# Raw second-layer weights requested before the zero fills, two start-up fills moved from VectorE to GpSimd, and activation tables touched early

## The chip, the core and the metric

The kernel runs on one core of a Trainium2 chip. The metric is the device time of one execution in microseconds, as the median of several runs. Beside the timed runs there is one profiled execution, from which every row below comes.

## The reference, cut to what matters

The input is `x` of 16 batches of 256 tokens with 128 channels, all in float32. Two layers follow one another. Each is "modulate, attention-like block, add back, modulate, expert block, add back".

```python
# layer 0, attention: 16 heads of 8 channels, causal softmax, a gate per token
logits = where(causal, einsum('bqhd,bkhd->bhqk', Q, K) * scale, -inf)
out = einsum('bhqk,bkhd->bqhd', softmax(logits) * gate, V) @ Wo + bo
# layer 0, expert block: plain attention over 256 tokens, then 8 experts, all used for every token
y = einsum('bse,bseh->bsh', softmax(x @ Wg + bg), relu(x @ W1 + b1) @ W2 + b2)
# layer 1, linear attention, with qkv_w, p1_w, p2_w (the "raw second-layer weights", used transposed)
kv = einsum('bhqd,bhqe->bhde', layernorm(k), layernorm(v)) / Q * temperature + attn_bias
h = gelu((q @ kv + x) @ p1_w.T + p1_b) @ p2_w.T + p2_b + x
# layer 1, expert block: top 2 of 8 experts with a capacity of 1024 slots each; rows beyond it are dropped
h = gelu(xb @ w1) @ w2        # xb: the rows gathered by slot; results are added back by token
```

## The kernel before, in words

All of the work is cut into named steps, such as `("up", n, e, f)`. A small planner inside the kernel file (`Plan`, `order_steps`) simulates the engines with a guessed cost for every part of a step (`work="sp:10 dma:6"` means ten microseconds of SyncE's queue and then six of a transfer), and writes down for every engine the order in which the parts were taken. The program of each engine is then those parts in that order. Each engine works strictly in its order and waits on semaphores in front of each part, so an early part that has to wait holds up all behind it. In the planner a part becomes available when all steps in its `after` have ended, 0.2 after the last of them. TensorE takes the available part of lowest rank. Every other queue takes the one with the smallest value of (time at which it became available minus `urgent`). Transfers don't compete with each other in the planner.

```python
for entry in sorted(queue, key=lambda q: (q[2].rank, q[1]) if ranked
                    else (q[0] - q[2].urgent, q[2].rank, q[1])):
```

The steps that matter here, in order of time:

- **Start.** VectorE fills the four `k_stack` tiles with -1 (`L1666`, semaphore `minus`), and only then begins its planned order with `moment(0)` (`L1739`), `stat(0,0,0)`, which needs the first quarter of `x` (`L1007`). GpSimd builds the constants and, in `masks()`, the causal masks (`L2520`).
- **Layer-0 attention.** ScalarE, VectorE (chunk 0) or GpSimd (later chunks, `L2589`, `L2594`) cut the projections into three bfloat16 pieces (`L1796` to `L1800`). SyncE writes them to memory (`write`, `L1047`) and reads them back in another layout (`stack(b, w)`, `L1059`; w = 0 is q, w = 1 is k). `max` (`L1247`, `L1263`) is the first TensorE work of a batch. `mrow(b)` sends the row maxima to the stack (`L1066`). `exp` and `pv` follow. Batch `b` uses tile `b % 4`.
- **Fills.** Four transfers zero the answer rows (`L1088`) and four the routed rows (`L1091`), about 1 MB each: steps `bg 4` to `bg 11`. The following SyncE parts are `wraw` (the raw second-layer weights, `L1098` to `L1100`), `mg_w(0)` (the first chunk's gate rows, out of `gT`, written to memory, `L1111`), `blk` (32 tiny transfers, `L1106` and `L1107`), `w1` (2 MB of expert weights, `L1128`) and `mg_r(0, 0)` (the gate rows read back, spread over the partitions, `L1122`). `mg_w(n)` first waits for `mg_t(n)`, ScalarE's copy into `gT` (`L2397`).
- **Layer-0 experts.** `up` (`L1454`), `down` (`L1487`), then `mix(n, e)` on VectorE (`L1965`), which needs the gate rows and frees a PSUM bank, and `acc` on GpSimd (`L2633`). Between them run the plain attention steps of later chunks and `wt(0)` to `wt(4)`, the transposes of the raw weights (`L1530`), then `wc` on VectorE. All of them are needed only by layer 1.
- **Layer 1.** Linear attention of chunk n overlaps the layer-0 experts of later chunks: `la_1` (`L2473`, Gelu), `la_2` (`L1582`), `la_c` (`L2479`), `la_x` (`L1590`); `rt_e` (`L2485`, Exp) begins the routing. When ScalarE's next function isn't in the table that is loaded, an ACT_TABLE_LOAD stands before the activation.

Of the kernel before, what the change touches and what calls it, by code (L numbers as in the profile page):

```python
# [12 lines left out]
ACT = mybir.ActivationFunctionType  # L13
# [3 lines left out]
B, S, C = 16, 256, 128  # L17
P = 128
# [10 lines left out]
NCH = TOK // CHUNK  # L29
CT = CHUNK // P  # L30
BPC = CHUNK // S
# [15 lines left out]
QR = 4  # L47
# [297 lines left out]
def order_steps():  # L345
    p = Plan()
# [88 lines left out]
    ROWS_AT = 9  # L435
    for b in range(B):
        for w in range(2):
            p.step("stack", b, w, work="sp:1.4 dma:2.0", urgent=3 if b < 2 else 0, after=[("write", b // BPC, w, b % BPC)]
                   + ([(("exp", b - QR, u), "pe") for u in range(6)] if b >= QR else []))
        for u in range(6):  # L440
            pair = p.buffer("pair")
            p.step("max", b, u, work=f"pe:{.52 if u < 2 else .42} dve:1.2", urgent=8 if b == 0 else 2, after=[("stack", b, 0), ("stack", b, 1), ("masks",)] + ([(("mrow", b - 2), "pe")] if b >= 2 else []), rank=10 * (6 * b + u - ROWS_AT) + 3,
                   opens=[(0, pair)], closes=[(1, pair)], pair=pair)
        bank = p.buffer("bank")
        p.step("mrow", b, work="pe:.32 act:.32 dve:.42 sp:1.15 dma:2.2", urgent=9 if b < 2 else 6, after=[("max", b, u) for u in range(6)]
               + ([("mrow", b - 2)] if b >= 2 else []), rank=10 * (6 * b - 4), opens=[(0, bank)], closes=[(2, bank)], bank=bank)
        for h in range(2):
            sums = p.buffer("bank")
            for v in range(3 * h, 3 * h + 3):
                u, pair, probs = EXPS[v], p.buffer("pair"), p.buffer("probs")  # L450
                p.step("exp", b, u, work=f"pe:{.42 if u < 4 else .52} act:.93", after=[("mrow", b)], rank=10 * (6 * b + v),
                       opens=[(0, pair), (0, probs)], closes=[(1, pair)], pair=pair, probs=probs)
                p.step("pv", b, v, work="pe:.5", after=[("exp", b, u), ("gv_v", (TPB * b + u // 4) // GT)]
                       + ([("pv", b, v - 1)] if v % 3 else []), rank=10 * (6 * b + v + 2) + 5,
                       opens=[(0, sums)] if v % 3 == 0 else [], closes=[(0, probs)], sums=sums, probs=probs)
            tile, bank = p.buffer("turned"), p.buffer("bank")
            p.step("oc", b, h, work="act:.53", after=[("pv", b, 3 * h + 2)], opens=[(0, tile)], closes=[(0, sums)], sums=sums,
                   turned=tile)
            p.step("turn", b, h, work="pe:.5 dve:.45", after=[("oc", b, h)], rank=10 * (6 * b + 3 * h + 6) + 1, opens=[(0, bank)],
                   closes=[(0, tile), (1, bank)], bank=bank, turned=tile)  # L460
# [17 lines left out]
    values_over = [gated, *[("gv_a", n) for n in range(NT // GT)]]  # L478
# [13 lines left out]
        p.step("free", n, work="sp:0", after=[("values_over",)], opens=[(0, t) for t in tiles])  # L492
        p.step("bg", n, work="sp:.8 dma:10", after=[("free", n)], first=tiles[0], second=tiles[1])
    for n in range(4, 12):
        p.step("bg", n, work="sp:.8 dma:9", after=[("mrow", B - 1)])


    def project_out(n, rank, chain):
# [79 lines left out]
    for e in range(NE):  # L578
        p.step("sw", 0, e, work="act:.53 dve:.62",
               after=[("bg", 0), ("bg", 1), last_pv] + [(("exp", 12 + e // 2, u), "pe") for u in range(6)])  # L580
# [27 lines left out]
        p.step("w2", h, work="sp:.5 dma:4", after=[(("down", NCH - 1, 2 * h + 1, FC - 1), "pe")]  # L608
               + ([("fetch", u) for u in range(2)] if h == 3 else []))

    p.step("wraw", work="sp:10 dma:6", after=[*values_over, ("mrow", B - 1)])
    for g in range(5):
        one("wt", g, "pe:.12 dve:.22", [("wraw",)], MOE - 60, (91, g, 0))
    p.step("wc", work="dve:2.5", after=[("wt", g) for g in range(5)] + [("mod", 1)])
# [122 lines left out]
def build(nc, a, out):  # L737
    ctx = ExitStack()
    with ctx:
        def sb(name, shape, dt=F32):  # L740
            return ctx.enter_context(nc.sbuf_tensor(name, shape, dt))

        def semaphore(name):
            return ctx.enter_context(nc.semaphore(name))

        p = order_steps()
# [3 lines left out]
        def sem(kind, by=None):  # L750

            stage, engines = SIGNALS[kind]
            return stage_sems[stage, by or engines.split()[-1]]
# [8 lines left out]
        def held(name, *step):  # L762
            return p.held[step, name].at
# [36 lines left out]
        def pair_of_tiles(i):  # L800
            if i < 4:
                return tmp[:, 2 * i:2 * i + 2, :]
            if i >= 8:
# [28 lines left out]
        result_out = semaphore("result_out")  # L832
        consts = semaphore("consts")
        IDENT, COUNTERS, ZEROS, VA_PAD, VA_ONES, EMPTY, MASKS = range(1, 8)
        minus = semaphore("minus")

        wqk = sb("wqk", [P, 2, C])
        wvd = sb("wvd", [P, VW])
# [1 line left out]
        magic = sb("magic", [P, 1])  # L840
        mixed_bias = sb("mixed_bias", [P, 1])
        least = sb("least", [P, 1])
        wo = sb("wo", [P, C])
        fw = sb("fw", [P, 4, C])
        wg = sb("wg", [P, NE])
# [8 lines left out]
                  for wh in range(2)]  # L854

        PLACES = ((slice(0, 3), slice(3, 6, 2), slice(4, 5)), (slice(2, 5), slice(0, 6, 5), slice(1, 2)))
        q_heads, k_heads = ([t[:, :, :].rearrange("p a t -> p (a t)").bitcast(BF16).rearrange("p (i t) -> p i t", i=IH)
                             for t in stacks] for stacks in (q_stack, k_stack))
# [16 lines left out]
        def col(name, i=0):  # L875
            return cols[:, COLS[name] + i:COLS[name] + i + 1]
# [126 lines left out]
        def _(eng):  # L1003
            w = Waits(eng)
# [45 lines left out]
            def stack(b, wh):  # L1050
                r, n = b % QR, b * S // CHUNK
                dst, src, sem_in = ((q_heads, q_pieces, q_in), (k_heads, k_pieces, k_in))[wh]
                w.wait_ge(minus, 1)
                if b >= QR:
                    for u in range(6):
                        w.wait_ge(*done("exp", b - QR, u, by="pe"))
                w.wait_ge(piece_out[wh][b % BPC], 16 * 3 * (n + 1))
                for j in range(2):
                    eng.dma_start(dst[r][HALF * j:HALF * j + DEEP, :, :].rearrange("p i t -> p (i t)"),  # L1059
                                  src[n, b % BPC, :, :, j, :, :].rearrange("s d i t -> (s d) (i t)")).then_inc(sem_in[r], 16)  # L1060
# [599 lines left out]
        def _(eng):  # L1660
            w = Waits(eng)
            chain = Tally(semaphore("vector_chain"))


            for r in range(QR):
                last = eng.memset(k_heads[r][:, :, :], -1.0)  # L1666
            last.then_inc(minus, 1)

# [18 lines left out]
                return eng.scalar_tensor_tensor(y, t, 1.5 * 0.375, y, ALU.add, ALU.mult)  # L1687

            eng.memset(least[:, :], EPS)
            eng.memset(magic[:, :], float(0x5F3759DF)).then_inc(chain.sem, chain.more())  # L1690
            w.wait_ge(chain.sem, chain.n)

# [534 lines left out]
        def _(eng):  # L2227
            w = Waits(eng)

            for name, at in COLS.items():  # L2230
# [5 lines left out]
                n = v.shape[0] // P  # L2236
# [232 lines left out]
            def la_1(b):  # L2469
                w.wait_ge(*done("la_1", b, by="pe"))  # L2470
                for c in cleared("tmp", "la_1", b):
                    w.wait_ge(*c)
                eng.activation(T(held("tmp", "la_1", b))[:, 0:S], psum[:, held("bank", "la_1", b), 0:S], ACT.Gelu,  # L2473
                               bias=col("L1_attn_p1_b")).then_inc(sem("la_1"), 1)

            def la_c(b):
                t = T(held("src", "la_c", b))[:, 0:S]
# [4 lines left out]
            def rt_e(g):  # L2482
                t = sc[:, g * RG:(g + 1) * RG, :]
                w.wait_ge(*done("rt_s", g))
                eng.activation(t, t, ACT.Exp).then_inc(sem("rt_e"), 1)  # L2485

            def rt_b(b):
                r = b % 2
# [26 lines left out]
        def _(eng):  # L2515
            w = Waits(eng)
# [15 lines left out]
            for t in range(NT // 8):  # L2532
                last = eng.memset(va[:, 8 * t:8 * t + 8, :, HD], 1.0)
# [5 lines left out]
            def masks():  # L2539
# [19 lines left out]
                for stage in stages:  # L2559
                    w.wait_ge(chain.sem, chain.n)  # L2560
                    for j in range(2):
                        last = stage(slice(HALF * j, HALF * (j + 1)))[-1]
                    if stage is not stages[-1]:
                        last.then_inc(chain.sem, chain.more())
                last.then_inc(consts, 1)
                w.wait_ge(consts, MASKS)

            def late():
                eng.dma_start(wo[:, :], a["L0_attn_Wo"]).then_inc(late_in, 16)
# [173 lines left out]
```

## Time and profile before

| | |
|---|---|
| median of 3 runs | 1013.37 us (1011.25 to 1015.28) |
| the profiled execution's own time | 1019.3 us |
| its span, first to last instruction | 1017.5 us |
| TensorE busy with matmuls | 936.2 us, 92% |
| VectorE, ScalarE, GpSimd busy | 608.9, 567.8, 347.9 us |
| mean granted TensorE clock | 0.963 |

The profiled execution is 1.8 us longer than its own span, and 5.9 us longer than the median. Times in the rows count from the start of the span. "Idle before" is the time that an engine had nothing to do just before an instruction, and the arrow names what ended it.

### The profile page before, as it was taken

Reading aid. Unit: us, or ns where it says so; the run is one execution under the profiler, and the core shown is the slowest. Engines: PE = TensorE matmul, PEld = TensorE weight load, DVE = VectorE, ACT = ScalarE, POOL = GpSimd, SP = SyncE. Lnnn points to the kernel's source line nnn. Section 1 sums busy time; section 2 is a strip of 40 time slices with the busy share of each in tenths; the row PEclk is TensorE's granted clock in tenths of the full one; section 3 lists DMA queues with packets and bytes.
Section 4 is the critical chain, followed back from the end, with each engine's and each line's share of the span. In section 5 each row is a group of like instructions: output and inputs, shape, how many; then the busy total and the mean of one; then the engine's idle time right before and its main releaser. Section 6 shows DMA issues by size and latency. Waiting matters only on the chain.

```text
span 1017.5 us, 17056 instructions
## 1 busy us (share of the span) xinstructions
PE 936.2 (92%) x6324; PEld 628.5 (62%) x6324; DVE 608.9 (60%) x1747; ACT 567.8 (56%) x965; POOL 347.9 (34%) x436
## 2 busy tenths in 40 slices
PE   4599889888988999999999999999999998988997
PEld 3355555545656787656666566666666666877983
DVE  8988778577475675355554535554455764747334
ACT  4477876775774565445465455545555565453430
POOL 4446540330000000233424443243533323457671
PEclk9599999989997999999999999999999998998999
DMA  5865342643593000101101111111101213112316
GB/s 136 205 156 133 101 122 66 157 123 141 123 226 125 23 22 3 43 21 52 53 22 63 42 40 44 47 37 42 62 21 53 73 47 97 44 50 72 107 46 227
DMA packets 86398, 83.10 MB, mean 82 GB/s; under 512 B 9202, under 2 KB 72680, under 8 KB 86316
## 3 DMA queue, kind: packets, MB, share of 16 engines
q1 hardware_dynamic: 81092, 73.32, 26.1%
q0 software_dynamic: 4320, 8.27, 2.5%
q8 instruction: 50, 0.82, 0.3%
q10 hardware_dynamic: 904, 0.42, 0.1%
q14 instruction: 32, 0.26, 0.1%
HBM read 50.53 MB, written 31.72 MB: 81 GB/s over the span
## 4 chain that ended last, share of the span: by engine, by line
PE 56%; DVE 13%; issue 10%; ACT 9%; SPq 5%; POOL 5%; DMA 2%; another core or an unknown queue 0%; POOLq 0%; DVEq 0%; ACTq 0%
PE psum L1454 13%; PE psum L1487 12%; PE psum L1477 4%; PE psum L1309 4%; PE psum L1247 3%; PE psum L1263 2%; PE psum L1290 2%; POOL routed L2691 2%; SPq L1091 2%; ACT ew L2323 1%; PE psum L1217 1%; PE psum L1239 1%; POOL hT L2633 1%; DVE maxes L1844 1%; PE psum L1368 1%
## 5 line engine op out<-in xcount | busy, mean ns | idle before, releaser
L2432 ACT ACTIVATE big<-psum,cols 128x512 f32<-128x512 f32 x256 | 173.8, 689 | 162.7 <-PE psum L1454 152.1
L1454 PE MATMUL psum<-parts,q_stack 128*128 128x512 f32 x640 | 260.2, 488 | 4.2 <-issue 2.3
L1487 PE MATMUL psum<-big,ew 128*128 128x512 f32 x512 | 249.5, 595 | 0.0
L2633 POOL TENSOR_TENSOR hT<-hT,gb_tok 128x512 f32<-128x512 f32 x56 | 73.6, 1315 | 289.5 <-DVE gb_tok L1965 289.1
L1454 PEld LDWEIGHTS psum<-parts,q_stack 128*128 128x128 f32 x640 | 113.4, 194 | 61.7 <-issue 50.1
L1844 DVE TENSOR_REDUCE maxes<-psum 128x4 f32<-128x1024 f32 (+1 forms) x96 | 114.8, 1218 | 27.6 <-PE psum L1263 27.3
L1487 PEld LDWEIGHTS psum<-big,ew 128*128 128x128 f32 x512 | 96.1, 190 | 53.2 <-issue 39.9
L1454 PE MATMUL psum<-parts,k_stack 128*128 128x512 f32 x320 | 127.5, 398 | 0.0
L1965 DVE SCALAR_TENSOR_TENSOR gb_tok<-psum,cols,gb_tok 128x512 f32<-128x512 f32 x64 | 47.9, 749 | 92.4 <-PE psum L1487 84.7
L2714 POOL DMA_INDIRECT answers<-hT,to x64 | 62.5, 976 | 54.7 <-DVE hT L2163 38.0
L2691 POOL DMA_INDIRECT routed<-big,slot_i x64 | 63.2, 988 | 41.8 <-DVE slot_i L2143 22.2
L1477 PEld LDWEIGHTS psum<-ew,big 128*128 128x128 f32 x512 | 67.8, 200 | 9.4 <-issue 3.2
L1477 PE MATMUL psum<-ew,big 128*128 128x128 f32 x512 | 68.9, 284 | 4.7 <-issue 2.6
L2439 ACT ACTIVATE big<-psum 128x512 f32<-128x512 f32 x64 | 38.2, 598 | 56.9 <-PE psum L1454 39.8
L1454 PEld LDWEIGHTS psum<-parts,k_stack 128*128 128x128 f32 x320 | 61.1, 191 | 13.9
L2323 ACT ACTIVATE ew<-psum 128x1024 f32<-128x1024 f32 x60 | 60.6, 1023 | 13.5 <-PE psum L1290 12.7
L2255 ACT ACTIVATE hT<-psum,modT 128x256 f32<-128x256 f32 x64 | 34.5, 565 | 33.9 <-PE psum L1217 33.7
L1247 PE MATMUL psum<-mask_qk,rows_qk 64*128 64x128 bf16 (+1 forms) x384 | 33.6, 256 | 21.2 <-DMA k_stack<-k_pieces 7.5
L2633 POOL TENSOR_TENSOR hT<-big,gb_tok 128x512 f32<-128x512 f32 x8 | 10.2, 1278 | 107.8 <-DVE gb_tok L1965 107.7
L2589 POOL TENSOR_TENSOR ew<-ew,gb_tok 128x512 f32<-128x512 f32 x14 | 16.1, 1155 | 85.6 <-ACT ew L2288 85.6
L2163 DVE TENSOR_SCALAR hT<-psum,big 128x128 f32<-128x128 f32 x64 | 18.4, 345 | 42.9 <-PE psum L1477 36.2
L1309 PE MATMUL psum<-ew,big 128*32 128x128 f32 (+1 forms) x640 | 41.2, 355 | 1.5 <-ACT ew L2323 1.1
(401 smaller groups left out, 1656.2 us busy)
## 6 DMA issues: line engine op xcount, KB each, us to landing
gb_tok<-gate_rows SPq DMA_DIRECT2D x32, 512.0 KB
q_stack<-q_pieces SPq DMA_DIRECT2D x32, 192.0 KB, 3.5
k_stack<-k_pieces SPq DMA_DIRECT2D x32, 192.0 KB, 4.5
routed<-empty_row SPq DMA_DIRECT2D x4, 1040.0 KB, 13.4
big<-routed SPq DMA_DIRECT2D x16, 260.0 KB
answers<-gb_tok SPq DMA_DIRECT2D x4, 1024.0 KB, 11.1
q_pieces<-gb_tok SPq DMA_DIRECT2D x16, 192.0 KB, 2.1
k_pieces<-gb_tok SPq DMA_DIRECT2D x15, 192.0 KB, 2.1
```

The lines of the kernel that those rows point to most:

```text
L1247: eng.matmul(bank(2 * s + j).rearrange("p (g k) -> p g k", k=width)[:, :, cs], rows_of[rs, half, :], mask[rs, 0:heads, :], start=half == 0 ...
L1309: last = eng.matmul(psum[QUAD * c:QUAD * (c + 1), bank_at, (g % 2) * S + kb * P:(g % 2 + 1) * S], va_flat[:, TPB * b + kb, at:at + QUAD], ...
L1454: last = eng.matmul(bank(i), w1_part(wp, e)[:, fs], parts[2 * xk + xp][:, :], start=n == 0, stop=n == 2)
L1477: last = eng.matmul(psum[:, i, k * C:(k + 1) * C], hid[:, r, f, k * P:(k + 1) * P], ew2[:, e, f, :], start=f == 0, stop=f == FC - 1)
L1487: eng.matmul(bank(i), ew2[:, e, f, :], hid[:, r, f, :], start=f == 0, stop=f == FC - 1).then_inc(sem("down", "pe"))
L1844: eng.tensor_reduce(maxes[:, b % 2, qb, :, ii[0]:ii[-1] + 1], psum[:, 2 * s:2 * s + 2, :].rearrange("p j (g k) -> p j g k", k=P * (qb + 1) ...
L1965: eng.scalar_tensor_tensor(tile, bank(held("bank", "mix", n, e)), col("L0_ffn_b2", e), tile, ALU.add, ALU.mult).then_inc(sem("mix"), 1)
L2323: eng.activation(pair_of_tiles(held("probs", "exp", b, u)), psum[:, 2 * s:2 * s + 2, :], ACT.Exp, scale=float(HD) ** -0.5).then_inc(sem("e ...
L2432: eng.activation(hid[:, held("hid", "up", n, e, f), f, :], bank(held("bank", "up", n, e, f)), ACT.Relu, bias=col("L0_ffn_b1", e * FC + f)) ...
L2633: eng.tensor_tensor(hT[:, ns], xpT[:, ns] if e == 0 else hT[:, ns], gate_wide[:, e // GHELD % 2, e % GHELD, :], ALU.add).then_inc(sem("acc ...
L2691: eng.indirect_dma_start(out=routed, out_offset=bass.IndirectOffsetOnAxis(ap=slot_i[:, k, t:t + 1], axis=0), in_=rows_buf[:, r, m, k, :], ...
L2714: eng.indirect_dma_start(out=answers, out_offset=bass.IndirectOffsetOnAxis(ap=to[:, k, m:m + 1], axis=0), in_=ans_buf[:, k, m, :], in_offs ...
```

## The change

Four things are changed.

1. `wraw` is planned with 1.5 instead of 10 microseconds of SyncE and with `urgent=20`, and each of the eight fills has `wraw` in its `after`.
2. The stacks of batch 0 have `urgent=9` instead of 3.
3. The fill of `k_stack` tiles 2 and 3 goes from VectorE's beginning to the end of GpSimd's `masks()`. It has a semaphore of its own, `minus_later`, on which the stacks of these two tiles wait.
4. ScalarE runs a two-element Exp after each odd `la_1` but the last, and a two-element Gelu after `rt_e(0)` to `rt_e(5)`, on a new small tile `ready`.

```diff
-            p.step("stack", b, w, work="sp:1.4 dma:2.0", urgent=3 if b < 2 else 0, after=[("write", b // BPC, w, b % BPC)]
+            p.step("stack", b, w, work="sp:1.4 dma:2.0", urgent=9 if b < 1 else 3 if b < 2 else 0, after=[("write", b // BPC, w, b % BPC)]
...
     for n in range(4, 12):
-        p.step("bg", n, work="sp:.8 dma:9", after=[("mrow", B - 1)])
+        p.step("bg", n, work="sp:.8 dma:9", after=[("mrow", B - 1), ("wraw",)])
...
-    p.step("wraw", work="sp:10 dma:6", after=[*values_over, ("mrow", B - 1)])
+    p.step("wraw", work="sp:1.5 dma:6", urgent=20, after=[*values_over, ("mrow", B - 1)])
...
+        ready = sb("ready", [P, 2])
...
-                w.wait_ge(minus, 1)
+                w.wait_ge(*((minus, 1) if r < BPC else (minus_later, 1)))
...
-            for r in range(QR):
+            for r in range(BPC):
                 last = eng.memset(k_heads[r][:, :, :], -1.0)
             last.then_inc(minus, 1)
...
+            eng.memset(ready[:, :], 0.0)
...
                                bias=col("L1_attn_p1_b")).then_inc(sem("la_1"), 1)
+                if b % BPC == BPC - 1 and b < B - 1:
+                    eng.activation(ready[:, 1:2], ready[:, 0:1], ACT.Exp)
...
                 eng.activation(t, t, ACT.Exp).then_inc(sem("rt_e"), 1)
+                if g < NCH - 2:
+                    eng.activation(ready[:, 1:2], ready[:, 0:1], ACT.Gelu)
...
                 w.wait_ge(consts, MASKS)
+                for r in range(BPC, QR):
+                    last = eng.memset(k_heads[r][:, :, :], -1.0)
+                last.then_inc(minus_later, 1)
```

Here `BPC` is 2, `QR` is 4, `B` is 16 and `NCH` is 8.

## Rows read from the trace of the kernel before

**Rows 1.** The page, part 1: busy time, share of the span, instructions.

```profile
span 1017.5 us, 17056 instructions
...
PE 936.2 (92%) x6324; PEld 628.5 (62%) x6324; DVE 608.9 (60%) x1747; ACT 567.8 (56%) x965; POOL 347.9 (34%) x436
```

**Rows 2.** Timeline 0 to 60 us: start, duration, engine, line, out<-in, [idle before <-releaser].

```profile
1.71 0.45 SPq L1007 DMA_DIRECT2D x<-in_L_attn_x  x1
...
2.28 0.73 POOL L2531 MEMSET big<- 128x736 f32 x1
...
9.56 0.49 DVE L1739 BATCH_NORM_STATS2 stats<-x 128x6 f32<-128x128 f32 x2
...
20.13 0.69 DVE L1796 TENSOR_TENSOR ew<-ew,gb_tok 128x512 f32<-128x512 f32 x1 [0.68 <-ACT ew L2288]
...
26.84 1.80 SPq L1059 DMA_DIRECT2D q_stack<-q_pieces  x4
...
29.02 2.27 POOL L2589 TENSOR_TENSOR ew<-ew,gb_tok 128x512 f32<-128x512 f32 x2 [15.41 <-ACT ew L2288]
29.11 1.09 DVE L1672 SCALAR_TENSOR_TENSOR drs<-drift,magic 128x8 int32<-128x8 int32 x1
...
35.67 0.61 PE L1247 MATMUL psum<-mask_qk,rows_qk 64*128 64x256 bf16 x4 [7.52 <-DMA k_stack<-k_pieces]
```

**Rows 3.** Instructions on tile k_stack: durations in ns min/median/max, first and last start.

```profile
L1666 DVE MEMSET k_stack<- x4: 1765/1765/1765, 1.3 to 7.7; 128x2048 bf16 x4
```

**Rows 4.** DMA issues, window 0 to 2.15 us: KB each, us from issue to landing.

```profile
x<-in_L_attn_x SPq DMA_DIRECT2D x1, 512.0 KB, 4.5
```

**Rows 5.** Timeline 262 to 330 us, all engines.

```profile
278.13 0.57 ACT L2397 COPY gT<-psum 8x512 f32<-8x512 f32 x1
...
304.28 0.48 PE L1530 MATMUL psum<-ident,big 128*128 128x128 f32 x1 [4.05 <-DMA big<-in_L_attn_p_w]
...
321.55 0.75 DVE L1965 SCALAR_TENSOR_TENSOR gb_tok<-psum,cols,gb_tok 128x512 f32<-128x512 f32 x1 [4.33 <-DMA gb_tok<-gate_rows]
...
322.45 0.85 PE L1217 MATMUL psum<-ident,tmp 128*128 128x128 f32 x6 [1.50 <-DVE gb_tok L1965]
...
324.42 1.19 PE L1454 MATMUL psum<-parts,q_stack 128*128 128x512 f32 x2 [1.12 <-DVE x L1874]
```

**Rows 6.** Timeline of SyncE's queue, 200 to 420 us.

```profile
267.76 0.41 SPq L1088 DMA_DIRECT2D answers<-gb_tok  x1
...
289.83 4.79 SPq L1091 DMA_DIRECT2D routed<-empty_row  x1
294.67 3.54 SPq L1098 DMA_DIRECT2D big<-in_L_attn_qkv_w  x1
...
300.22 0.33 SPq L1111 DMA_DIRECT2D gate_rows<-gT  x1
...
311.67 0.40 SPq L1128 DMA_DIRECT2D ew<-in_L_ffn_w  x1
```

**Rows 7.** The chain that ended last, 260 to 335 us: start, duration, what.

```profile
312.17 9.27 DMA gb_tok<-gate_rows
```

**Rows 8.** Windows of 5 us: busy per engine, then TensorE clock, DMA share, GB/s.

```profile
305.00:310.00 5.00, 5.00 (x12) 3.19 (x11) 1.46 (x5) 1.08 (x3) 0.00 (x0) 0.50 0.02 1
...
325.00:330.00 5.00, 5.00 (x16) 4.03 (x15) 4.66 (x24) 3.57 (x8) 0.00 (x0) 0.50 0.01 3
```

**Rows 9.** Groups by line and form, ScalarE: busy us, mean ns, idle before.

```profile
L2473 ACT ACT_TABLE_LOAD x8 | 10.3, 1283 | 0.1
```

**Rows 10.** Timeline 445 to 530 us, around the first two linear-attention chunks.

```profile
452.08 0.70 PE L1582 MATMUL psum<-tmp,w_t 128*128 128x256 f32 x2 [0.84 <-ACT tmp L2473]
...
453.62 0.59 ACT L2479 ACTIVATE tmp<-tmp,small,modT 128x256 f32<-128x256 f32 x1
...
454.77 0.38 PE L1590 MATMUL psum<-ident,tmp 128*128 128x128 f32 x2
...
514.06 0.70 PE L1582 MATMUL psum<-big,w_t 128*128 128x256 f32 x2 [0.56 <-ACT big L2473]
```

More of the change, by code:

```diff
@@ L834, in build @@
         IDENT, COUNTERS, ZEROS, VA_PAD, VA_ONES, EMPTY, MASKS = range(1, 8)
-        minus = semaphore("minus")
+        minus, minus_later = semaphore("minus"), semaphore("minus_later")
         wqk = sb("wqk", [P, 2, C])
```

## The prediction, made before the result was known

> **What bounds the kernel now.** I read the page first. TensorE is busy for 936.2 of 1017.5 us [rows 1], and after the first 60 us it has few gaps, so a gap taken away or added there reaches the end nearly whole. The edits touch three stretches, and in each I looked for what ends the gap.
>
> At the start the timeline [rows 2] shows VectorE at work without a pause. Its first planned instruction is at 9.56, behind four fills of 1.765 us [rows 3]. TensorE stands still for 7.52 us until 35.67, when the k stack of batch 0 lands. The view of that chain runs back over SyncE's issues from 26.84 on and over the pieces to VectorE at 9.56: the beginning of VectorE sets it, not TensorE.
>
> At the fills there are two gaps. TensorE waits 4.05 us for the raw weights, until 304.28. Then VectorE's `mix(0,0)` waits 4.33 us for the gate rows and starts at 321.55, and TensorE has gaps of 1.50 and 1.12 us on its account [rows 5]. The second is the one that counts: the chain that ended last passes through SyncE's whole row of fills, raw weights and tiny transfers, and over the gate transfer, landing at 312.17 + 9.27 = 321.44 [rows 6, 7]. What TensorE loses to the raw weights is lost only until it has run out of work that doesn't need the gates. So the question for this stretch is when the gate rows land.
>
> In layer 1 the reader should see small gaps before `la_2`, 0.84 us in the first chunk, behind table loads of 1.283 us [rows 9, 10].
>
> **The change part by part.**
>
> *The first batch's stacks first.* In the planner SyncE is free at 23.81 and takes `stack(0,0)`. At 25.21 it is free again. Then `stack(1,0)` is available (since 24.91) and `stack(0,1)` isn't: its `write` ends at 26.02. The next choice, at 26.61, falls on `stack(0,1)` with either urgency. The order stays q0, q1, k0, k1, as the trace has it (two q stacks, four issues, from 26.84 before the first k stack) [rows 2]. Value 0. Had the order become q0, k0, k would be issued 0.9 us earlier (half of 1.80), which is the bound.
>
> *Two fills to GpSimd.* VectorE is free two fills earlier, each 1.765 plus 0.38 between them, 4.3 us in all; it would be ready at about 5.3. But `moment(0)` needs the first quarter of `x`, issued at 1.71 (issue 0.45) and landing 4.5 later [rows 2, 4]: 6.2 to 6.7, take 6.5. Gain 9.56 - 6.5 = 3.1. On GpSimd a fill of 736 elements takes 0.73 [rows 2], so 2048 take about 2.0, two of them 4.0, from 13.6 (29.02 - 15.41 [rows 2]) to 17.6. Its next work is then due at about 26, so nothing of GpSimd waits, nor do the stacks of tiles 2 and 3. VectorE could: a VectorE instruction that took 0.17 elsewhere took 1.09 beside GpSimd's tensor operation at 29.02 [rows 2]. VectorE's slack before the first cut into pieces is 0.68 (20.13 [rows 2]). The four fills of VectorE all took the same 1.765 although GpSimd filled beside only the first ones [rows 3], so I take 0.2 for contention and keep 2 fills of 2.0 less 0.68, 3.3, as its bound. Value -2.9, bounds -4.3 and +0.2. The `ready` fill is under 0.1.
>
> For this contention the Trainium skill ("SBUF — State Buffer", section "Who interferes with whom") has a rule: whichever starts first, a GpSimd operation or a VectorE copy or tensor_scalar in a two-port mode, holds the shared ports for the whole instruction, while tensor_tensor collides only with GpSimd's reads. By the rule a long fill on GpSimd could stop VectorE's copies for 2 us each, and the gain would be near 0; by the row of equal fills it is 2.9. The row at 29.11 agrees with the lock itself.
>
> *Raw weights ahead of the fills.* This needs the order of SyncE, which the planner fixes. In the planner of before `mrow(15)` ends at 240.13, the fills are taken from there, and `mg_w(0)` becomes available at 247.70. Nothing earlier changes, so these two stand. Now `wraw` is taken at 240.13: 1.5 of SyncE, 0.2, 6 of transfer, 0.2, ended at 248.03. The fills become available only then. `mg_w(0)` is available 0.33 before them, at an idle SyncE, and is taken first. The new order is therefore `wraw`, **`mg_w(0)`**, eight fills, `blk`, `w1`, `mg_r(0,0)`; before it was fills, `wraw`, `mg_w(0)`, `blk`, `w1`, `mg_r(0,0)`.
>
> On the chip `mg_w(0)` waits for ScalarE's copy into `gT`, which ends at 278.13 + 0.57 = 278.70 [rows 5] and depends on nothing that moved. Behind it on SyncE now stand all eight fills, which began at 267.76 [rows 6]. `wraw` alone takes three issues of about 0.45 with nothing queued, so SyncE is at the wait by 269.2 and stands there for 9.5 us. The count, all from [rows 6]:
>
> - The first fill moves from 267.76 to about 279.1: +11.3.
> - From the first to the end of the last fill it was 294.62 - 267.76 = 26.9, paced by the transfers. The same.
> - `wraw` and `mg_w(0)` no longer stand behind the fills: 300.55 - 294.67 = -5.9.
> - `blk` and `w1` as before.
>
> Sum +5.4: the gate rows are asked for at 317.6 instead of 312.17 and land at 326.9. The fills' landing isn't later than that: 267.76 to 304.2 was 36.5 us with the raw weights in it, so 279.1 + 35.5 = 314.6.
>
> The raw weights are there from about 275, and the 4.05 us gap goes, with the half-clock stretch behind it (0.50 in 305 to 310 [rows 8]). But TensorE then only runs out of work sooner, by some 6 to 7 us, and waits at the same place for gates that are 5.4 later. After the wait it has a half-clock stretch as it had before (0.50 in 325 to 330), so that cancels. Value of this part +5.4.
>
> *The order around it.* The planner believes that the gates come earlier: fills at 248.3 to 254.7, `blk` to 265.7, `mg_r(0,0)` at 265.8 instead of 268.2. So `mix(0,0)` becomes available about 1 earlier, at 273.1 instead of 274.2, and passes `stat(0,1,4)` (3.2 long in the planner, available at about 274). VectorE's order has `mix(0,0)`, and TensorE's the first step that needs its bank, with up to 5 us less of other work ahead of them. Each microsecond of such work that is moved behind the late gates is one more gap. From 0 to +5; I take +2, since banks and not VectorE often decide. The five transposes and `wc` go earlier and cost the same. The orders after this point are all shuffled; for that I add 3 us to either side.
>
> *Tables.* Without the load, `la_1` is 1.28 sooner. TensorE shows 0.84 of gap in the first chunk and 0.56 in the second [rows 10], and two more chunks have a gap like the second's. But `la_1(0)` follows the gates' Exp and keeps its load; only chunks 1 to 6 gain. The Exp after the odd `la_1` puts 1.28 + 0.2 on ScalarE where `la_c` of the even batch stands in half of the chunks: at 453.62 it started right after the odd `la_1`, and TensorE wants its result at 454.77 [rows 10]. It would come at 453.7 + 1.5 + 0.6 = 455.8, a gap of 1.0. So: chunks 1, 3 and 5 gain 0.8 each, 6 gains about 1; chunk 0 loses 1.0, chunks 2 and 4 lose 0.5 each: -3.4 + 2.0 = -1.4. Bounds: no loss, -4; no gain, +3. `rt_e` sooner by up to 1.28 meets no gap of TensorE.
>
> The Trainium skill ("ScalarE: Activation LUTs", section "What ACT_TABLE_LOAD costs") puts a switch at 2.66 us, load and drain. By it the gains and the losses here would double, to -2.8. The trace shows the load's 1.283 [rows 9] and the activation right behind.
>
> **The sum.** -2.9 + 5.4 + 2 - 1.4 = +3.1 us. On the profiled execution, 1019.3, that is 1022.4; on the median of the runs, 1013.37, it is 1016.5. A difference of 0.5%, 5.1 us, is about what a measurement of this kernel can tell.
>
> **The rivals.**
>
> - *The gates aren't late (faster).* If `mg_w(0)` stands behind the fills, SyncE loses 1.4 to `wraw` at the front and gains 5.5 behind: gates 4.1 earlier. With the start and tables: -4.1 - 2.9 - 1.4 = -8.4, 1005. The point that decides is 0.33 of planner time between `mg_w(0)` and the fills. My derivation excludes it, but a slip there is possible, or late gates that hit less work than I think.
> - *More work behind the gates (slower).* The reorder costs its 5 instead of 2, and the start gives only 1 because of GpSimd's fills: -1 + 5.4 + 5 - 1 = +8.4, 1022. For it: TensorE's gaps at 322 and 324 come directly from `mix(0,0)` and what is behind it. Against: with VectorE held up, much of the other work was already prepared.
> - *The start doesn't move.* The weights or the second quarter of `x` come too late; then +6.0, 1019.4. Against: TensorE waited 7.52 at 35.67 for this chain alone.
> - *All of it is hidden or cancels:* layer 1 absorbs the delay in its own gaps, within 2 us of 1013.4.
>
> **How the numbers follow.** Forecast (1012.5 to 1019, start gained, gates late) 0.46; gates not late 0.13; more work behind the gates 0.20; start unmoved 0.09; all cancels 0.12. The range reaches down to 1006, into the first rival, and up to 1024, past the second. Slower by over 0.5% begins at 1018.4: the second rival, most of the third and a part of the forecast's upper side, 0.36. Faster ends at 1008.3: the first rival and a little of the shuffle, 0.15. Same 0.49.
>
> **What would show it.** VectorE's first `L1739` at about 6.5, and TensorE's first `L1247` at about 32.8, still after q0, q1, k0, k1. SyncE: `L1098` at 267.8 - 2.9 = 265, `L1111` behind it at about 276, the first `L1088` after that. `L1530` with no gap. The first `L1965` at about 324, with over 7 us of VectorE's and TensorE's idle time before it. Eight `L2473` loads become two, and `L1590` has new gaps. The prediction is wrong if `L1111` stands behind the fills, or if TensorE has no long gap before the first `L1965`.

## The result, and the profile after

| | before | after |
|---|---|---|
| median of the runs | 1012.31 us (4 runs, 1011.23 to 1015.28) | 1024.27 us (4 runs, 1022.33 to 1025.69) |
| the profiled execution, its span | 1019.3, 1017.5 us | 1025.69, 1023.9 us |
| mean granted TensorE clock there | 0.963 | 0.968 |

The ratio is 1.0126, with a 95% interval of 1.0098 to 1.0155: the change makes the kernel 1.3% slower, 12 us. The forecast was 1016.5, that is 3.1 us slower, with a range of 1006 to 1024.

The two profiled spans differ by 6.4 us only. That of before was made in an execution 7 us above its median, so nothing below rests on the difference of these two spans. The kernel before was profiled a second time for that (first experiment). Line numbers shift by 1 or 2 with the change: `L1247` is now `L1248`, `L1454` `L1455`, `L1965` `L1967`, `L1111` `L1112`.

Page of the changed kernel, part 1, beside [rows 1]:

```profile
span 1023.9 us, 17061 instructions
...
PE 931.1 (91%) x6324; PEld 624.7 (61%) x6324; DVE 607.5 (59%) x1746; ACT 569.2 (56%) x978; POOL 351.9 (34%) x438
```

TensorE has the same 6324 matmuls and is no busier than before (931.1 us for 936.2). What was lost is idle time. The timeline of SyncE's queue, which answers to [rows 6] (start, duration, what is issued):

```profile
261.22 0.41 SPq L1099 DMA_DIRECT2D big<-in_L_attn_qkv_w  x1
...
262.20 0.44 SPq L1101 DMA_DIRECT2D big<-in_L_attn_p_w  x1
272.19 0.30 SPq L1112 DMA_DIRECT2D gate_rows<-gT  x1
272.53 0.40 SPq L1089 DMA_DIRECT2D answers<-gb_tok  x1
...
293.54 4.23 SPq L1092 DMA_DIRECT2D routed<-empty_row  x1
297.81 3.02 SPq L1107 DMA_DIRECT2D tcol<-in_L_attn_temperature  x1
...
311.77 0.39 SPq L1129 DMA_DIRECT2D ew<-in_L_ffn_w  x1
312.27 0.98 SPq L1123 DMA_DIRECT2D gb_tok<-gate_rows  x2
```

This is the order that the prediction had: raw weights, `mg_w(0)`, eight fills, `blk`, `w1`, gates. SyncE stands from 262.6 to 272.19 at the gate write (`L1112`), and the fills begin behind it. TensorE and VectorE, timelines, beside [rows 5]:

```profile
276.09 0.27 PE L1531 MATMUL psum<-ident,big 128*128 128x128 f32 x1
...
316.72 1.12 PE L1401 MATMUL psum<-ident,tmp 128*128 128x128 f32 x4 [12.79 <-DVE tmp L1909]
...
322.13 2.08 PE L1390 MATMUL psum<-tmp 128*128 128x256 f32 x4 [3.01 <-DVE gb_tok L1967]
```

```profile
312.68 0.29 DVE L1992 TENSOR_SCALAR wqk<-wqk,tcol 128x128 f32<-128x128 f32 x1 [14.22 <-DMA wqk<-in_L_attn_attn_bias]
...
321.32 0.75 DVE L1967 SCALAR_TENSOR_TENSOR gb_tok<-psum,cols,gb_tok 128x512 f32<-128x512 f32 x1 [4.66 <-DMA gb_tok<-gate_rows]
```

The first transpose of the raw weights no longer waits (4.05 us before). But TensorE has two gaps of 12.79 and 3.01 us on account of VectorE, which stands first at `blk` (`L1992`, 14.22 us), for the 32 tiny transfers, and then at `mix(0,0)` (`L1967`, 4.66 us), for the gates. Windows of 5 us, beside [rows 8] (busy us of TensorE, its weight loads, VectorE, ScalarE, GpSimd; then the granted clock):

```profile
305.00:310.00 5.00, 0.00 (x0) 0.00 (x0) 0.00 (x0) 0.00 (x0) 0.00 (x0) 0.92 0.02 0
310.00:315.00 5.00, 0.00 (x0) 0.00 (x0) 2.11 (x14) 0.00 (x0) 0.00 (x0) 0.50 0.37 114
315.00:320.00 5.00, 2.40 (x7) 1.58 (x7) 1.49 (x8) 1.27 (x2) 0.00 (x0) 0.50 1.03 381
320.00:325.00 5.00, 2.87 (x7) 2.33 (x8) 3.68 (x11) 0.00 (x0) 1.27 (x1) 0.50 0.35 141
325.00:330.00 5.00, 5.00 (x25) 4.34 (x24) 3.88 (x20) 2.92 (x9) 0.00 (x0) 0.88 0.00 0
```

For five microseconds no compute engine does anything, and the work behind the gap begins at the lower of the two clocks (0.50, 1.2 GHz).

### The profile page after: what moved, and what is told of

It is laid out like the page before. It is cut to its first block, busy times and chain, and to the rows that moved or that the text cites. A ratio compares the mean times of both kernels' runs of the same rounds, so it can differ in the third digit from the quotient of the medians.

```text
span 1023.9 us, 17061 instructions
## 1 busy us (share of the span) xinstructions
PE 931.1 (91%) x6324; PEld 624.7 (61%) x6324; DVE 607.5 (59%) x1746; ACT 569.2 (56%) x978; POOL 351.9 (34%) x438
## 4 chain that ended last, share of the span: by engine, by line
PE 58%; DVE 13%; issue 9%; ACT 8%; SPq 4%; POOL 4%; DMA 3%; another core or an unknown queue 0%; DVEq 0%; POOLq 0%; ACTq 0%
PE psum L1455 14%; PE psum L1488 13%; PE psum L1310 4%; PE psum L1478 3%; PE psum L1248 3%; PE psum L1264 2%; PE psum L1291 2%; ACT ew L2325 1%; SPq L1092 1%; PE psum L1412 1%; PE psum L1218 1%; PE psum L1324 1%; PE psum L1390 1%; POOL hT L2642 1%; PE psum L1240 1%
## 5 line engine op out<-in xcount | busy, mean ns | idle before, releaser
L1455 PE MATMUL psum<-parts,q_stack 128*128 128x512 f32 x640 | 263.5, 493 | 9.0 <-ACT big L2434 3.5
L1455 PEld LDWEIGHTS psum<-parts,q_stack 128*128 128x128 f32 x640 | 113.3, 193 | 69.4 <-issue 52.1
L1455 PE MATMUL psum<-parts,k_stack 128*128 128x512 f32 x320 | 127.4, 398 | 0.0
L1967 DVE SCALAR_TENSOR_TENSOR gb_tok<-psum,cols,gb_tok 128x512 f32<-128x512 f32 x64 | 47.9, 749 | 106.0 <-PE psum L1488 91.9
L1455 PEld LDWEIGHTS psum<-parts,k_stack 128*128 128x128 f32 x320 | 61.0, 191 | 14.0
L1248 PE MATMUL psum<-mask_qk,rows_qk 64*128 64x128 bf16 (+1 forms) x384 | 32.9, 252 | 22.1 <-ACT ew L2325 8.4
```

Source lines behind the costliest of these rows:

```text
L1248: eng.matmul(bank(2 * s + j).rearrange("p (g k) -> p g k", k=width)[:, :, cs], rows_of[rs, half, :], mask[rs, 0:heads, :], start=half == 0 ...
L1455: last = eng.matmul(bank(i), w1_part(wp, e)[:, fs], parts[2 * xk + xp][:, :], start=n == 0, stop=n == 2)
L1967: eng.scalar_tensor_tensor(tile, bank(held("bank", "mix", n, e)), col("L0_ffn_b2", e), tile, ALU.add, ALU.mult).then_inc(sem("mix"), 1)
```

## The experiments

Runs that were made together share their runs of the kernel before, whose median was 1017.17 us for the first four, 1008.47 for the next four and 1008.29 for the last four. So only ratios are compared across them. The profile of each is one execution.

### The parts one by one

**The kernel before, once more.**

> This is the kernel before, unchanged, profiled once more. In its first profile SyncE's first fill went out at 267.76, in the profile of the changed kernel its first transfer at that place (the raw weights) at 261.22, although every engine has the same order up to there apart from the two fills of the start. Theory A, the executions differ by themselves: the first profiled execution of the kernel before took 1019.3 us, 7 above its median of 1012.3, and lost those 7 in the attention phase. Then here the time is 1011 to 1015 and the first fill goes out at 261 to 264, so the whole 12 us of the change lie behind 262. Theory B, the change earned the 6.5 us in the attention phase: the first fill is at 267 to 268 here too.

It took 1016.58 us (span 1014.8). Timelines of SyncE, and below it TensorE:

```profile
264.70 0.41 SPq L1088 DMA_DIRECT2D answers<-gb_tok  x1
...
285.94 4.15 SPq L1091 DMA_DIRECT2D routed<-empty_row  x1
290.13 3.12 SPq L1098 DMA_DIRECT2D big<-in_L_attn_qkv_w  x1
...
295.03 0.29 SPq L1106 DMA_DIRECT2D tcol<-in_L_attn_temperature  x1
...
306.62 0.98 SPq L1122 DMA_DIRECT2D gb_tok<-gate_rows  x2
```

```profile
298.86 0.33 PE L1530 MATMUL psum<-ident,big 128*128 128x128 f32 x1 [1.68 <-DMA big<-in_L_attn_p_w]
316.82 1.51 PE L1217 MATMUL psum<-ident,tmp 128*128 128x128 f32 x6 [4.05 <-DVE gb_tok L1965]
```

The first fill is at 264.70, where it had been at 267.76. That is the end of the attention phase, and this place lies between 262.50 and 267.76 in the nine profiles of this study without the two fills on GpSimd (mean 264.69), and between 261.22 and 268.40 in the five with them (mean 264.24; there the first of fills or raw weights is counted). So the 6.5 us by which the changed kernel was ahead at 262 were mostly the scatter of executions, as theory A said, though the time came out 1.6 above the 1011 to 1015 that it gave, and the first fill 0.7 behind its 261 to 264.

**Two fills to GpSimd, alone.** The `minus_later` part of the diff on the kernel before.

> The kernel before with one part alone: two of the four k_stack fills go from VectorE to GpSimd, with their own semaphore. Theory A, the start is worth nothing: in the changed kernel TensorE's first L1248 came 1.5 us sooner (34.17 for 35.67), but its first L1310 at 59.4 came no sooner than before (59.1), because VectorE's maxima set the pace: within 1.5 us of the kernel before. Theory B, it is a gain of its own, later in the attention phase: 3 to 6 us faster. Theory C, the fills on GpSimd slow VectorE: 2 to 4 us slower.

Ratio 1.0011 (0.9992 to 1.0030): nothing, theory A. VectorE and GpSimd in its timeline, and then VectorE in the second profile of the kernel before:

```profile
6.23 0.49 DVE L1739 BATCH_NORM_STATS2 stats<-x 128x6 f32<-128x128 f32 x2 [1.01 <-DMA x<-in_L_attn_x]
...
14.57 1.00 DVE L1710 TENSOR_SCALAR means<-means 128x2 f32<-128x2 f32 x1
15.61 1.76 DVE L1713 TENSOR_SCALAR wvd<-wvd,means 128x64 f32<-128x64 f32 x1
...
19.04 0.16 DVE L1772 SCALAR_TENSOR_TENSOR shift<-mv,rstd 128x4 f32<-128x4 f32 x1
...
13.75 3.57 POOL L2568 MEMSET k_stack<- 128x2048 bf16 x2
```

```profile
16.81 0.17 DVE L1710 TENSOR_SCALAR means<-means 128x2 f32<-128x2 f32 x1
17.02 0.25 DVE L1713 TENSOR_SCALAR wvd<-wvd,means 128x64 f32<-128x64 f32 x1
...
19.11 0.16 DVE L1772 SCALAR_TENSOR_TENSOR shift<-mv,rstd 128x4 f32<-128x4 f32 x1
```

VectorE begins 3.3 us sooner, is still 2.24 ahead at `L1710`, and 0.07 ahead at `L1772`. Two tiny instructions take 1.00 and 1.76 us instead of 0.17 and 0.25. They end at 15.57 and 17.37. GpSimd's two fills, at half of 3.57 each, end at 15.54 and 17.32. `batch_norm` work beside the same fills, between 13.75 and 14.5, took its usual time. Some of the head start did survive: VectorE's first cut into pieces (`L1796`) was at 19.57 beside 20.12, and SyncE issued the k stack at 28.13 beside 28.64. But TensorE's first `L1247`, which waits for this transfer, was at 34.58, beside 34.51. From its issue on the k stack took 6.4 us here, 5.9 in the second profile of the kernel before and 7.0 in the first, so what was left was lost in the scatter of its landing.

The Trainium skill ("SBUF — State Buffer", section "Who interferes with whom") says that a VectorE tensor_scalar in a two-port mode is blocked for the whole of a GpSimd instruction that was issued first. These rows agree with it to 0.05 us.

**The tables, alone.**

> The kernel before with one part alone: the two kinds of one-column activations that load the tables ahead. Theory A, they don't count: between -2 and +2 us. Theory B, the 3.5 us that the changed kernel lost between 887 and 993 us come from them: 3 to 5 us slower. In either case 8 loads at the Gelu of la_1 become 2, and small gaps before la_2 shrink while others open at L1591.

Ratio 1.0027 (1.0006 to 1.0047), 2.7 us slower: between the two theories. Timeline of TensorE (the first of three rows of each kind: the one in chunks 0, 2 and 4, the other in chunks 1, 3 and 5), and of ScalarE:

```profile
449.39 0.44 PE L1591 MATMUL psum<-ident,tmp 128*128 128x128 f32 x2 [0.85 <-ACT tmp L2483]
...
525.20 0.73 PE L1455 MATMUL psum<-parts,q_stack 128*128 128x512 f32 x2 [0.77 <-ACT big L2434]
```

```profile
447.35 1.28 ACT L2478 ACT_TABLE_LOAD   x1
448.64 0.20 ACT L2478 ACTIVATE ready<-ready 128x1 f32<-128x1 f32 x1
448.75 0.58 ACT L2483 ACTIVATE tmp<-tmp,small,modT 128x256 f32<-128x256 f32 x1
...
523.07 1.28 ACT L2491 ACT_TABLE_LOAD   x1
524.37 0.20 ACT L2491 ACTIVATE ready<-ready 128x1 f32<-128x1 f32 x1
524.48 0.67 ACT L2434 ACTIVATE big<-psum,cols 128x512 f32<-128x512 f32 x1
```

The Exp loaded ahead stands in front of `la_c`, which TensorE waits for: 3 x 0.85. The Gelu loaded ahead stands in front of an `up` activation. This came at 522.59 in the second profile of the kernel before and comes at 524.48 here, of which 0.6 is the offset of the two at this place: 3 x 0.77. What is saved is three gaps of 0.56 at `la_2`. Sum 2.55 + 2.31 - 1.68 = +3.2 us, and 2.7 was measured.

**The raw weights, alone.** The two planner lines of `wraw` and of the fills.

> The kernel before with one part alone: the raw weights ahead of the fills, urgency 20 and 1.5 us in the planner, fills behind them. Theory A, this part is the whole loss: 9 to 13 us slower, 1021 to 1025, with VectorE standing at blk (L1990) for over 10 us and TensorE for over 8 us behind it. Theory B, it is half of it, the rest comes from the tables or the start: 4 to 7 us slower. The forecast on record had +7.4 for this part (gates late 5.4, order 2).

Ratio 1.0097 (1.0071 to 1.0123), 9.8 us slower: theory A. The planner gives every engine the same order here as in the changed kernel, so this run holds all of the change's reordering. SyncE, TensorE and VectorE in its timeline:

```profile
275.73 0.40 SPq L1088 DMA_DIRECT2D answers<-gb_tok  x1
...
296.57 4.43 SPq L1091 DMA_DIRECT2D routed<-empty_row  x1
301.05 3.01 SPq L1106 DMA_DIRECT2D tcol<-in_L_attn_temperature  x1
...
315.49 0.98 SPq L1122 DMA_DIRECT2D gb_tok<-gate_rows  x2
```

```profile
319.76 1.11 PE L1400 MATMUL psum<-ident,tmp 128*128 128x128 f32 x4 [12.63 <-DVE tmp L1907]
325.60 2.08 PE L1389 MATMUL psum<-tmp 128*128 128x256 f32 x4 [3.45 <-DVE gb_tok L1965]
```

The attention phase ended at the same time in this profile as in the second one of the kernel before (264.4 and 264.7), so the two can be laid side by side. The gates are asked for 315.49 - 306.62 = 8.9 us later and take the same 9.3 to `mix(0,0)`. TensorE's gaps from 262 to 345 sum to 16.7 instead of 6.7: +10.0.

### Which wait costs

**VectorE's `blk` behind `mix(0,0)`.** On the changed kernel:

```diff
-    p.step("blk", work="pool:1.2 sp:11 dma:5 dve:.3", ...
+    p.step("blk", work="pool:1.2 sp:11 dma:20 dve:.3", ...
```

> The changed kernel, with blk's transfers put into the planner as 20 us instead of 5, so that VectorE's blk stands behind mix(0,0) instead of ahead of it. SyncE's order is that of the changed kernel. Theory A, the gate rows set the loss: VectorE no longer stands 14 us at blk, but TensorE runs out of work all the same, and the gates land at 321 to 325; ratio to the kernel before 1.008 to 1.014. Theory B, VectorE's place of blk sets it: 5 to 9 us of the 12 come back, ratio 1.002 to 1.007, with the gates landing as late.

Ratio 1.0146 (1.0108 to 1.0183), just above theory A's 1.014: nothing comes back. TensorE's timeline has one gap where there were two:

```profile
325.96 2.07 PE L1369 MATMUL psum<-hT,fw 128*128 128x256 f32 x4 [18.64 <-DVE gb_tok L1967]
```

The 14 us at `blk` are gone, the longest wait of this stretch in the changed profile, and the time is no shorter: TensorE had run out of work that doesn't need the gates. The gates were asked for 1.4 us later after the end of the attention phase than in the changed kernel (315.73 less 263.31, beside 312.27 less 261.22), so a gain of that size could be hidden here, but not one of 5 to 9 as theory B had it.

**Fills that don't wait.** The kernel before with only the planner line of `wraw` changed:

```diff
-    p.step("wraw", work="sp:10 dma:6", after=[*values_over, ("mrow", B - 1)])
+    p.step("wraw", work="sp:1.5 dma:6", urgent=20, after=[*values_over, ("mrow", B - 1)])
```

> The kernel before with the raw weights first (urgency 20, 1.5 us) but fills that don't wait for them: SyncE's order is raw weights, eight fills, mg_w(0), blk, gates, w1 instead of raw weights, mg_w(0), eight fills, blk, w1, gates. This is the first rival on record (gates not late). Theory A, mg_w(0) ahead of the fills is what costs: no stand of SyncE for ScalarE's copy, fills begin 1.4 later than before instead of 11, gates at the time of the kernel before or up to 6 earlier (they are ahead of the 2 MB here): ratio 0.990 to 1.002. Theory B, the reordering of VectorE's and TensorE's work by the early raw weights is what costs: ratio 1.006 or more here too.

Ratio 0.9967 (0.9944 to 0.9990), 3.3 us faster, theory A. Beside 1.0097 with the dependency this is 13 us for one word of the planner. That the early raw weights reorder the other engines, as they do here too, is not what costs. The word moves more than SyncE's queue, though. By the planner `mix(0,0)` has seven more steps in front of it on VectorE than with the dependency, and `blk` three fewer. In the profile `mix(0,0)` no longer waits for the gates, and TensorE's one long gap comes from `blk`, at which VectorE stood 8.38 us:

```profile
310.28 0.69 PE L1217 MATMUL psum<-ident,big 128*128 128x128 f32 x2 [7.73 <-DVE big L1782]
```

So what the gates' lateness costs is read from the run before this one, and this run shows that it goes with the dependency.

**The changed kernel with that word taken back.**

```diff
-        p.step("bg", n, work="sp:.8 dma:9", after=[("mrow", B - 1), ("wraw",)])
+        p.step("bg", n, work="sp:.8 dma:9", after=[("mrow", B - 1)])
```

> The changed kernel with one word taken back: the fills don't wait for the raw weights. All the rest of the change stays, the tables and the start too. Theory A (the fills behind mg_w(0) are 12 to 14 of the loss, the tables 3, the start 0 to 1): ratio 0.998 to 1.003, with gates at about 310 instead of 321. Theory B, other parts of the change carry the loss when together: ratio over 1.006.

Ratio 1.0029 (1.0011 to 1.0048): theory A. Of the 12.6 thousandths of the change, 9.7 are the fills behind the raw weights. What is left has the size of the tables, but that is a coincidence in part. Every engine has the same order as in the run above, which gained 3.3 thousandths. With start and tables (1.1 and 2.7) the sum would be 1.0005, and 2.4 thousandths more were measured. The intervals allow this, and no run explains it. VectorE stands 8.00 us at `blk` in this profile too. SyncE in its timeline:

```profile
296.81 3.15 SPq L1112 DMA_DIRECT2D gate_rows<-gT  x1
...
310.93 0.83 SPq L1123 DMA_DIRECT2D gb_tok<-gate_rows  x2
```

### Towards a better version

**Gates asked for first**, on the kernel before, nothing of the change in it:

```diff
-    p.step("w1", work="sp:.1 dma:12", after=[("sw", 0, e) for e in range(NE)])
+    p.step("w1", work="sp:.1 dma:12", after=[("mg_r", 0, 1)] + [("sw", 0, e) for e in range(NE)])
...
-    p.step("blk", ..., after=[..., last_pv])
+    p.step("blk", ..., after=[..., last_pv, ("mg_r", 0, 0), ("mg_r", 0, 1)])
```

> The kernel before, with mg_r(0,0) and mg_r(0,1) ahead of w1 and of blk on SyncE; nothing of the change in it. In the second profile of the kernel before the gates were asked for at 306.6 and landed at 315.9, behind 11.1 us of tiny transfers and a transfer of 2 MB. Theory A: asked for when the fills have landed, about 299, landing at 302 to 305; TensorE's 4.5 us of gap at 317 go, and part of a half-clock stretch behind: 3 to 8 us faster, ratio 0.992 to 0.997. Theory B, other work and not the gates is short there: within 2 us.

Ratio 0.9948 (0.9925 to 0.9971), 5.2 us faster. The gates are asked for at 299.38 instead of 306.62, and `mix(0,0)` waits for TensorE and not for them, as VectorE's timeline shows:

```profile
305.51 0.75 DVE L1965 SCALAR_TENSOR_TENSOR gb_tok<-psum,cols,gb_tok 128x512 f32<-128x512 f32 x1 [3.14 <-PE psum L1487]
```

**The same with the raw weights first.**

> The last one, with mg_r(0,0) and mg_r(0,1) ahead of blk and w1 as well. Theory A: raw weights at once and gates at 300 to 306: neither the gap of 1.7 to 4 us before the first transpose of the raw weights nor the one before mix(0,0): 6 to 11 us faster than the kernel before, ratio 0.989 to 0.994. Theory B, as in the others: within 2 us or slower.

Ratio 0.9978 (0.9960 to 0.9997), 2.2 us faster: nearer to theory B, and no better than with the gates alone. The gap had moved, as TensorE's timeline shows:

```profile
319.32 1.02 PE L1438 MATMUL psum<-wg,big 128*128 128x8 f32 x4 [4.28 <-DVE big L1925]
```

VectorE stood 5.84 us at `blk` just before. Here, with the gates early, `blk` is the wait that comes last, as in the two runs with free fills above.

**Gelu ahead, no Exp**, on the kernel before.

> The kernel before with the Gelu loaded ahead behind rt_e, and without the Exp behind la_1. Where both are loaded ahead, TensorE waited 0.85 us three times before L1591 and 0.77 three times before L1455, both behind the Exp's load, and no longer 0.56 three times before L1583. Theory A: those six gaps go and the gain stays: 1 to 3 us faster than the kernel before, ratio 0.997 to 0.999. Theory B, it is not the Exp but the changed rhythm of ScalarE: ratio 1.001 to 1.004 as with both.

Ratio 1.0010 (0.9995 to 1.0025): no gain, so theory A falls, but the measurement doesn't tell it from the pair either. The rows say why: the gaps of 0.85 at `L1591` are gone, but those of 0.77 at `L1455` stay (523.97, 645.97, 767.99), since they belong to the Gelu's load.

**Both**, gates first and Gelu ahead, on the kernel before.

> The kernel before with the gate reads ahead of blk and of the 2 MB (0.9948 alone) and the Gelu ahead. Theory A, the two add up: ratio 0.991 to 0.994, and faster than either kernel of this case. Theory B, no more than with the gates alone: 0.994 to 0.996.

Ratio 0.9928 (0.9906 to 0.9950). The interval holds both theories.

**The changed kernel, mended.** Fills free, gates first, `blk` late as above, no Exp ahead.

> The changed kernel, mended by what the runs showed: fills no longer behind the raw weights, gate reads ahead of the 2 MB and of blk, blk put into the planner late so that VectorE takes it behind mix(0,1), and of the tables only the Gelu ahead. In the run with raw weights and gates first VectorE stood 5.8 us at blk and TensorE 4.3 us behind it. Theory A, that wait goes: 7 to 11 us faster than the kernel before, ratio 0.989 to 0.993. Theory B, TensorE's gaps there are already bought back later: ratio 0.994 to 0.998 as in its neighbours.

Ratio 0.9878 (0.9859 to 0.9896), 996.02 us beside 1008.29: 12 us faster than the kernel before, a little more than the 7 to 11 of theory A, and the fastest of all. SyncE's queue in its timeline, and windows over the place of the former gaps:

```profile
293.64 3.14 SPq L1112 DMA_DIRECT2D gate_rows<-gT  x1
301.75 0.82 SPq L1123 DMA_DIRECT2D gb_tok<-gate_rows  x2
```

```profile
310.00:320.00 10.00, 10.00 (x56) 8.20 (x55) 8.81 (x40) 6.72 (x22) 0.00 (x0) 1.00 0.28 88
320.00:330.00 10.00, 10.00 (x64) 8.71 (x64) 6.56 (x20) 6.13 (x17) 1.28 (x1) 1.00 0.13 54
```

TensorE's gaps from 262 to 345 sum to 0.8 us, and it keeps its full clock. In the run with raw weights and gates first the same windows show 5.72 and 10.00 us of work at a clock of 0.88 and 0.77. Between these two runs `blk`'s place, the Gelu and the start differ together; that `blk`'s place is the larger part is read from the gap that is gone, and was not run alone.

## Why the prediction was wrong

The mechanism of the largest term was right: `mg_w(0)` slipped ahead of the fills, and the late gate rows made the loss. But that term was too small by 2.4 us, and in the two others, which had been forecast as gains, a step failed. The parts, each alone, against their terms (ratio less one, by 1012.31; intervals in brackets):

| term | forecast | measured alone |
|---|---|---|
| start | -2.9 (-4.3 to +0.2) | +1.1 (-0.8 to +3.0) |
| raw weights: gates late, order around it | +5.4 + 2 | +9.8 (7.2 to 12.5) |
| tables | -1.4 (-4 to +3) | +2.7 (0.6 to 4.8) |
| sum | +3.1 | +13.6; the whole change +12.8 (9.9 to 15.7) |

All three terms were too favourable, by 4.0, 2.4 and 4.1 us. The tables' +2.7 lies within the bounds of its term, and the start's interval reaches into the bounds of its own. It is the three together that leave the range.

- **Stacks first: right.** The planner gives every engine the same order with either urgency (the changed kernel and the raw weights alone have equal orders), and the four issues follow q0, q1, k0, k1 in the profile.
- **Start: the step that failed is the contention of 0.2**, what VectorE was to lose beside GpSimd's fills. The beginning was right (6.13 and 6.23 for 6.5). But four equal fills on VectorE [rows 3] said nothing of copies and tensor_scalars beside a long fill on GpSimd. Of the 3.3 us, 2.2 went at these two fills (2.24 ahead at `L1710`, 0.07 at `L1772`) and the rest in small pieces before them, while GpSimd still built the masks. The bound of 3.3, and the page's rule with a gain near 0, were closer. The row at 29.11 [rows 2], 1.09 for 0.17, had been the one to weigh. What the start would be worth without this contention was not run. The 35.67 from which the term was counted was itself a late landing: the same kernel had 34.51 in its second profile.
- **Gates late: the right count with one wrong entry.** Against the second profile of before: the first fill +11.0 (forecast +11.3); the fills themselves -0.1 (0); `wraw` and `mg_w(0)` no longer behind them -4.9 (-5.9); `blk` and `w1` **+2.9** ("as before"). Sum +8.9 for +5.4. The 3.54 us of the raw weights' first issue [rows 6] were not theirs: whatever is issued right behind the last fill pays them. It was taken off as a saving, and came back at `blk`'s first transfer of a few bytes, 3.01 us for 0.29. With free fills the gate write paid it, 3.15.
- **Order around it: about 1 of 2, and not resolved.** It is 9.8 less 8.9, and the interval of the 9.8 is 7.2 to 12.5. The reading behind the term was wrong: in the planner of the changed kernel `mix(0,0)` doesn't pass `stat(0,1,4)`, which stays ahead of it. The place of `blk` on VectorE, not named in the forecast, gave the longest wait in the changed kernel, and moving it brought nothing back.
- **Tables: the step that failed is where the loads go.** The gain was 3 x 0.56, not 3 x 0.8 and 1.0 for chunk 6, where the second profile of the kernel before has no gap at `la_2`. The Exp cost 3 x 0.85 = 2.55 for 2.0. The Gelu behind `rt_e` was costed at nothing, with `rt_e` "sooner by up to 1.28" as its only effect, and cost 3 x 0.77, because an `up` activation stands behind it on ScalarE. The Trainium skill ("ScalarE: Activation LUTs", section "What ACT_TABLE_LOAD costs") puts a switch at 2.66 us with a drain. In the rows above the activation begins at 448.64, 0.01 after a load of 1.28, and a gap of 0.85 or 0.77 is less than one load: these rows show the load alone, and the measurement decides.
- **The rivals.** "More work behind the gates", 1022, came nearest, but by luck: its order term of 5 was some 4 too high, and that made up in part for gates, tables and start, which were 3.5, 3.7 and 2.1 too low (5.4 for 8.9, -1 for +2.7, -1 for +1.1). "Gates not late" was tried as fills that don't wait. It gained 3.3 us alone, where -4.1 had been given, and with start and tables it was 2.9 slower, where -8.4 had been given. Its gates were asked for 42.9 us after the end of the attention phase (308.48 less 265.57), not 4.1 sooner than the 41.9 of before (306.62 less 264.70). The same wrong entry is in this count: the gate write behind the last fill took 2.90 us for 0.34, and the fills themselves took 27.3 for 25.4. The rows landed about 4 us sooner all the same, for a reason that the rival didn't have: here they are asked for ahead of the 2 MB, and took 4.0 to 4.9 us from issue to landing for 9.3. But `mix(0,0)` waited for them no longer, so the gain of 3.3 isn't shown to be theirs.

What stays open: in the stretch from 850 to 950, TensorE's gaps sum to between 7.2 and 15.7 us in the profiles of this study, also in two kernels whose timelines agree to a microsecond up to 843 (13.2 in the second profile of the kernel before, 7.2 with the Gelu ahead). A part of it belongs to the execution and not to the kernel. In the profile with 13.2, 10.0 us are waits that nothing in the profile ends (`<-issue`), the longest 6.5 before `L1477` at 918.37. Such waits, 2.3 to 10.0 us in all, stand there in the six profiles of the first comparison and of the first four runs, and in none of the eight later ones, with whose runs the kernel before was 4 to 9 us faster too. What they are is not shown. Without them the gaps of this stretch still vary from 2.8 to 13.3, and whether the change moves them was not tried. The sum of the parts doesn't need it.

## What to carry to other kernels

A transfer put ahead of a row of large ones is free only if nothing that waits for an engine slips in between: follow each queue to its first wait, and see what stands behind it. Take the time of an issue behind large transfers as a property of the place and not of the transfer. A load, a fill or a dummy instruction "in idle time" costs what the next instruction of the same engine is waited for, so name that instruction, and of two long waits in a row ask what ends the last, before the first is mended. Once the last is mended, look again: with the gates early, the wait at `blk` that had cost nothing was the one left.

## What the runs showed of the hardware

- An issue on SyncE took 0.4 us on its own and, from the third of the eight 1 MB transfers on, 2.9 to 5.6. The first one behind them took 3.12 for 192 KB, 3.15 for 16 KB and 3.01 for some bytes (2.9 to 3.5 in all profiles). The next took 0.3 to 1.5.
- A GpSimd fill of 2048 bfloat16 columns took 1.785 us, about what VectorE's took (1.765). VectorE's tensor_scalars beside it, of 2 and 64 columns, lasted until it ended.
- The gate rows took 9.3 us to arrive behind a transfer of 2 MB. Issued ahead of it at 299.38, they landed within 5.1 and were there before `mix(0,0)` at 305.51.
- An activation began 0.01 us after a table load of 1.28. A load ahead of its use delayed what stood behind it: TensorE waited 0.85 us in three chunks for the Exp and 0.77 in three for the Gelu, and got back 0.56 in three.
